# Expert rows weighted on eviction and added into the residual by scatter, in place of a gather and mix of chosen rows

## The chip, the cores and the metric

The program runs on one core of one Trainium2 chip, in float32 (some matmul operands are float32r or bfloat16). The metric is the device time of one execution in microseconds (us). The kernel before took 609.7 us, the median of three runs (607.96 to 610.41).

## The reference

The input is one sequence of 2048 tokens of width 128. Four residual blocks follow one another, each on a layer norm of the running sum:

```python
x = x + attn_a(layernorm(x))     # 16 heads, element-wise decaying state, a scan over the tokens
x = x + ffn(layernorm(x))        # mixture of experts, first pass
x = x + attn_b(layernorm(x))     # linear attention with exp features
x = x + ffn(layernorm(x))        # mixture of experts, second pass, same weights
```

The change is in `ffn`. It routes each token to 2 of 8 experts, each with room for 640 tokens; a token beyond that is dropped for that expert:

```python
logits = xt @ w_g
top_v, top_i = top_k(logits, 2)
probs  = softmax over the two chosen logits          # = sigmoid of their difference, both ways
rank   = running count of tokens per expert; kept if rank < 640
h      = gelu(batch[e] @ c_fc[e])                    # 640x128 @ 128x512
y      = h @ c_proj[e]                               # 640x512 @ 512x128
out[t] = sum over the (at most) 2 kept experts of probs * y[slot of t]
```

## The kernel before

Engine programs are written by hand, one list of instructions for each engine, and they meet at semaphores. The order on each queue is the order in the code. Tokens stand in 16 tiles of 128 (four chunks of four tiles); `xres` in SBUF is the running sum.

A pass of the mixture of experts (k = 0 or 1) goes so:

- **Routing.** For each chunk VectorE (DVE) picks the two experts (`choose`, which also writes `gap`, the difference of the two top logits), TensorE counts ranks, DVE makes slot numbers (`locate`).
- **Dispatch.** GpSimd (POOL) scatters the normed rows with 32 indirect DMAs (L447) into `slots_x[k]` in DRAM. A row holds 128 numbers and the number of the place in `chosen_y` where its result belongs. Slots that no token takes keep the number 65536, which the result's scatter skips.
- **Experts.** For each of 8 experts SyncE (SP) loads the 640 rows (`xe`), TensorE turns them and multiplies, ScalarE (ACT) does the Gelu, and DVE copies the result from PSUM to `ye` (L932). POOL scatters it with 5 indirect DMAs of 128 rows into `chosen_y` in DRAM (L477). `xe`, `ye` and `y_to` have two buffers.
- **Combination.** When all 80/2 = 40 scatters of the pass have landed, SP loads `chosen_y` back into `got` with 8 DMAs (L332), two for each chunk. DVE multiplies each tile of `got` by `weight` and adds it to `xres`, two instructions for each tile (`mix`, L941 and L946). `weight` comes from `probabilities` (ACT) and `weights` (DVE, with the matmul `totals`).

After pass 0 the second attention starts: `stats_chunk` and `norm_chunk` on DVE, `turn_chunk` (L1267) and `project` on TensorE, and then the features, where TensorE, ACT and DVE are all busy. ACT's features begin behind `act.wait_ge(mixed, NT)` (L670). After pass 1 SP waits for all of `mixed` and stores `xres` to `out` with one DMA (L356).

Of the kernel before, what the change touches and what calls it, by code (L numbers as in the profile page):

```python
# [46 lines left out]
ROW = D + 1  # L47
# [23 lines left out]
def program(nc, x, Wq, Wk, Wv, Wbeta, Wg, Wout, ln_g, ln_b, W_qkv, proj, W_out, b_out, w_g, c_fc, c_proj, out):  # L71
# [8 lines left out]
    with ctx:  # L80
# [29 lines left out]
        chosen_y = nc.dram_tensor("chosen_y", [KT * P, D], F32).ap()  # L110
# [38 lines left out]
        with ExitStack() as mb:  # L149
# [9 lines left out]
            gap = sb("gap", [P, NT], F32, mb)  # L159
            prob = sb("prob", [P, KT], F32, mb)  # L160
# [7 lines left out]
            limits = sb("limits", [P, NT, NE], F32, mb)  # L168
            limit = sb("limit", [P, NT], F32, mb)
            kept = sb("kept", [P, KT], F32, mb)  # L170
            weight = sb("weight", [P, KT], F32, mb)
# [7 lines left out]
            got = sb("got", [P, KT, D], F32, m)  # L179
            projf = got[0:3 * GR, 0:NT, :].rearrange("p (g t) d -> p g (t d)", g=NG)  # L180
# [24 lines left out]
        slots_clear, y_clear = sem("slots_clear"), sem("y_clear")  # L205
# [17 lines left out]
        logit_mm, logit_used, route_step, gap_ready, prob_ready = (  # L223
            sem(n) for n in ("logit_mm", "logit_used", "route_step", "gap_ready", "prob_ready"))
        chosen_ready, carry_ready, rank_mm, rank_used, index_ready, limit_mm, limit_used, weight_ready, scattered = (
            sem(n) for n in ("chosen_ready", "carry_ready", "rank_mm", "rank_used", "index_ready", "limit_mm",
                             "limit_used", "weight_ready", "scattered"))
# [4 lines left out]
        rows_made, ids_made, y_to_ready = sem("rows_made"), sem("ids_made"), sem("y_to_ready")  # L232
        got_in = [sem(f"got_in{c}") for c in range(NB)]
        mix_first = sem("mix_first")
        pstklo_ready = sem("pstklo_ready")
        mixed = sem("mixed")
# [17 lines left out]
        out_t = out.rearrange("a (t p) d -> p (a t) d", p=P)  # L254
# [18 lines left out]
        def _(sp):  # L273
# [21 lines left out]
            for j in range(0, KT, 4):  # L295
                sp.dma_start(chosen_y[j * P:(j + 4) * P, :].rearrange("(j p) d -> p j d", p=P),
                             empty_rows[:, 0:4, 0:D]).then_inc(y_clear, 16)

            def experts(k):

                if k == 0:
                    sp.wait_ge(xres_a, NB)
                else:
                    for c in range(NB):
                        sp.wait_ge(stk_in[c], 2 * 16 * 3 * NG)
                sp.dma_start(cfc_sb[:], c_fc.rearrange("e d f -> d e f")).then_inc(cfc_in, 16)
                if k == 0:
                    sp.wait_ge(zeroed, 2)
                    for r in range(3):
                        for a_ in range(GH):  # L310
                            row = GR * r + HD * a_
                            sp.dma_start(projf[row:row + HD, :, a_ * F:(a_ + 1) * F],
                                         proj.rearrange("(g a) d f -> a d g f", a=GH)[a_]).then_inc(proj_in, 16)
                sp.wait_ge(scattered, 16 * KT * (k + 1))
# [40 lines left out]
            sp.wait_ge(mixed, 2 * NT)  # L355
            sp.dma_start(out_t, xres[:]).then_inc(stored, 16)  # L356
# [4 lines left out]
        def _(pool):  # L361
            pool.memset(empty_rows[:, :, 0:D], 0.0)
            pool.memset(empty_rows[:, :, D:ROW].bitcast(I32), int(FAR)).then_inc(zeroed, 1)
# [72 lines left out]
            def experts(k):  # L436

                if k == 0:
                    pool.wait_ge(xres_a, 1)
                    pool.iota(rows_x[:, :, D].bitcast(I32), [[P, KT]], base=0,  # L440
# [30 lines left out]
                pool.wait_ge(y_clear, 16 * KT // 4)  # L471
                for e in range(NE):
                    b = e % 2
                    pool.wait_ge(y_to_ready, k * NE + e + 1)
                    pool.wait_ge(ye_ready, k * NE + e + 1)
# [18 lines left out]
        def _(act):  # L494
# [108 lines left out]
            def probabilities(k):  # L603
                act.wait_ge(gap_ready, NB * (k + 1))
                act.activation(prob[:, 0:NT], gap[:], ACT.Sigmoid).then_inc(prob_ready, 1)
                act.activation(prob[:, NT:KT], gap[:], ACT.Sigmoid, scale=-1.0).then_inc(prob_ready, 1)

# [4 lines left out]
            def experts(k):  # L612
                probabilities(k)
                for e in range(NE):
                    b = e % 2
                    s = k * NE + e
                    if s == 2:
                        stack_proj()
# [51 lines left out]
            act.wait_ge(mixed, NT)  # L670
# [33 lines left out]
        def _(dve):  # L704
# [115 lines left out]
            def choose(k, c, lg):  # L820
# [3 lines left out]
                for kk, src in enumerate((lg, lg2[:])):  # L824
# [5 lines left out]
                    if kk == 0:  # L830
# [7 lines left out]
                dve.tensor_tensor(gap[:, TB * c:TB * c + TB], top[:, 0, :], top[:, 1, :],  # L838
                                  ALU.subtract).then_inc(gap_ready, 1)
# [26 lines left out]
            def weights(k, totals):  # L866
                dve.wait_ge(limit_mm, k + 1)
                by_tile = chosen[:, :, 1, :, :].rearrange("p c e t -> p c t e")
                dve.tensor_tensor(limits[:].rearrange("p (c t) e -> p c t e", t=TB), by_tile,
                                  totals.unsqueeze(1).unsqueeze(1).broadcast_to((P, NB, TB, NE)),  # L870
                                  ALU.mult).then_inc(limit_used, 1)
                dve.wait_ge(limit_used, k + 1)
                link(dve.tensor_reduce(limit[:], limits[:], AX_X, ALU.add))
                dve.tensor_tensor(kept[:, NT:KT].rearrange("p (c t) -> p c t", t=TB), place[:, :, 3, :],
                                  limit[:].rearrange("p (c t) -> p c t", t=TB), ALU.is_ge)
                link(dve.tensor_single_scalar(kept[:, 0:NT].rearrange("p (c t) -> p c t", t=TB), place[:, :, 1, :],
                                              float(CAP), ALU.is_lt))
                dve.wait_ge(prob_ready, 2 * k + 2)
                dve.tensor_tensor(weight[:], prob[:], kept[:], ALU.mult).then_inc(weight_ready, 1)

# [24 lines left out]
            def experts(k, n):  # L905
                weights(k, ps[:, n, 2 * P:2 * P + NE])
# [10 lines left out]
                for e in range(NE):  # L917
# [9 lines left out]
                    if s >= 2:  # L927
                        dve.wait_ge(ye_out[b], 16 * NS * (s // 2))
                    dve.wait_ge(xe_in[b], 16 * (s // 2 + 1))
                    dve.tensor_copy(y_to[:, b, :], xe[:, b, :, D].bitcast(I32)).then_inc(y_to_ready, 1)  # L930
                    dve.wait_ge(ye_mm, s + 1)
                    dve.tensor_copy(ye[:, b, :], flat(ps[:, 6:8, :])[:, 0:NS * D]).then_inc(ye_ready, 1)  # L932

            def mix(k, c):
                if c == 0:
                    dve.wait_ge(weight_ready, k + 1)
                dve.wait_ge(got_in[c], 32 * (k + 1))

                def second(t):
                    dve.wait_ge(mix_first, k * NT + t + 1)  # L940
                    dve.scalar_tensor_tensor(out=xres[:, t, :], in0=got[:, NT + t, :],  # L941
                                             scalar=weight[:, NT + t:NT + t + 1], in1=xres[:, t, :],
                                             op0=ALU.mult, op1=ALU.add).then_inc(mixed, 1)

                for t in range(TB * c, TB * c + TB):
                    dve.scalar_tensor_tensor(out=xres[:, t, :], in0=got[:, t, :], scalar=weight[:, t:t + 1],  # L946
                                             in1=xres[:, t, :], op0=ALU.mult, op1=ALU.add).then_inc(mix_first, 1)
                    if t % TB:
                        second(t - 1)
                second(TB * c + TB - 1)  # L950

            experts(0, NB - 1)

            def stats_chunk(c):
                for t in range(TB * c, TB * c + TB):
                    dve.wait_ge(mixed, t + 1)
# [20 lines left out]
            mix(0, 0)  # L977
            stats_chunk(0)
            for c in range(NB):
                if c + 1 < NB:  # L980
                    mix(0, c + 1)
# [82 lines left out]
            experts(1, 5)  # L1064
            for c in range(NB):
                mix(1, c)
# [3 lines left out]
        def _(pe):  # L1070
# [137 lines left out]
            def totals(k, bank):  # L1208
                pe.wait_ge(carry_ready, (k + 1) * (NB + 1))
# [235 lines left out]
```

## Time and profile before

| | |
|---|---|
| median of three runs | 609.7 us (607.96 to 610.41) |
| the profiled execution | 607.78 us |
| its span in the profile | 606.1 us |
| busy: TensorE / VectorE / ScalarE / GpSimd | 390.6 / 301.9 / 237.9 / 225.7 us |
| chain of work that ended last | TensorE 41%, VectorE 13%, issue 8%, GpSimd 6%, ScalarE 5%, DMA 5% |
| eight experts of pass 0, first scatter to last landing | 236.9 to 309.3 us |
| eight experts of pass 1, first scatter to last landing | 515.5 to 588.0 us |

The profiled execution is 1.7 us longer than its span, and 1.9 us shorter than the median of the runs. Times in rows count from the start of the span. SPq is the queue on which SyncE issues DMAs. A DMA_INDIRECT row of POOL is the time in which it issues one scatter; the transfer comes behind it.

### The profile page before, as it was taken

To read this page: it belongs to the slowest core of one execution; us is meant where nothing else is said; L and a number is where in the kernel's file an instruction comes from. 1 tells how busy PE (TensorE), PEld (TensorE's weight loads), DVE (VectorE), ACT (ScalarE), POOL (GpSimd) and SP (SyncE) were. 2 spreads that over 40 slices of the span, in tenths; PEclk is the share of its full clock that TensorE was granted. 3 is DMA by queue.
4 is the path that set the end of the run, shared out by engine and by line. 5 is a ranking of instruction groups with operands and counts; after the bars stand their busy time and mean duration, and the time that the engine had idled before them with its cause. 6 is when DMAs were issued, how large, how long until landed. Compare 5 with 4: busy or idle time off the path is not lost.

```text
span 606.1 us, 6501 instructions
## 1 busy us (share of the span) xinstructions
PE 390.6 (64%) x2202; PEld 261.1 (43%) x2202; DVE 301.9 (50%) x711; ACT 237.9 (39%) x328; POOL 225.7 (37%) x245
## 2 busy tenths in 40 slices
PE   3737677557340029999807899975777209999920
PEld 2435444225230018888604533332444107888710
DVE  5486999837550001132139699878675501111105
ACT  2835333255240004323203799876745302332300
POOL 4002898800066692465423100000531550645540
PEclk9959897887555559999957999999775557999975
DMA  7950000000311121221051433330100120222016
GB/s 199 359 182 2 1 1 0 0 1 1 138 40 48 44 66 38 68 77 48 24 156 41 104 96 96 97 127 1 36 17 19 35 78 22 55 72 72 29 58 175
DMA packets 36289, 41.27 MB, mean 68 GB/s; under 512 B 5664, under 2 KB 23712, under 8 KB 36256
## 3 DMA queue, kind: packets, MB, share of 16 engines
q1 hardware_dynamic: 31648, 32.42, 18.4%
q0 software_dynamic: 4608, 8.44, 4.1%
q8 instruction: 18, 0.29, 0.2%
q14 instruction: 15, 0.12, 0.1%
HBM read 17.68 MB, written 17.90 MB: 59 GB/s over the span
## 4 chain that ended last, share of the span: by engine, by line
PE 41%; DVE 13%; issue 8%; POOL 6%; ACT 5%; DMA 5%; SPq 1%; POOLq 0%; DVEq 0%; ACTq 0%
PE ps L1072 38%; POOL slots_x L447 5%; DVE feat L997 3%; DMA slots_x<-rows_x,put_at 2%; PE ps L1223 2%; ACT expo L655 1%; DMA got<-chosen_y 1%; DVE xres L946 1%; DVE xres L941 1%; DMA xe<-slots_x 1%; DVE stats L807 1%; ACT rows_x L591 1%; ACT L655 1%; DMA chosen_y<-ye,y_to 1%; PE ps L1183 1%
## 5 line engine op out<-in xcount | busy, mean ns | idle before, releaser
L447 POOL DMA_INDIRECT slots_x<-rows_x,put_at x64 | 62.8, 981 | 166.1 <-DVE put_at L856 119.2
L477 POOL DMA_INDIRECT chosen_y<-ye,y_to x80 | 79.3, 992 | 94.2 <-DVE ye L932 68.3
L623 ACT ACTIVATE hT<-ps 128x640 f32<-128x640 f32 x64 | 45.0, 703 | 162.5 <-PE ps L1072 162.5
L997 DVE SCALAR_TENSOR_TENSOR feat<-expo,ps 128x1024 f32<-128x1024 f32 x64 | 76.8, 1216 | 11.5 <-ACT expo L655 11.1
L1072 PE MATMUL ps<-xeT,cfc_sb 128*128 128x320 f32 x256 | 75.8, 451 | 1.8 <-DVE xeT L914 1.8
L655 ACT ACTIVATE expo<-ps,minus_one 128x1024 f32<-128x1024 f32 x64 | 70.2, 1114 | 11.8 <-PE ps L1072 7.8
L1072 PE MATMUL ps<-cproj_sb,hT 128*128 128x128 f32 x640 | 74.6, 275 | 0.3
L1072 PEld LDWEIGHTS ps<-cproj_sb,hT 128*128 128x128 f32 x640 | 73.0, 192 | 0.9 <-ACT hT L623 0.6
L914 DVE COPY xeT<-ps 128x640 f32<-128x640 f32 x16 | 13.2, 824 | 120.0 <-PE ps L1223 120.0
L1072 PEld LDWEIGHTS ps<-xeT,cfc_sb 128*128 128x128 f32 x256 | 47.8, 199 | 24.0 <-ACT hT L623 6.5
L1223 PE MATMUL ps<-ident,xe 128*128 128x128 f32 x80 | 12.5, 292 | 57.0 <-DMA xe<-slots_x 57.0
L932 DVE COPY ye<-ps 128x640 f32<-128x640 f32 x16 | 13.2, 824 | 64.0 <-PE ps L1072 64.0
L424 POOL TENSOR_TENSOR read<-state,qT 128x1024 f32<-128x1024 f32 x16 | 38.1, 2379 | 9.9 <-DVE state L784 9.7
L784 DVE TENSOR_TENSOR_SCAN state<-decay,state,ps 128x1024 f32<-128x1024 f32 x16 | 37.5, 2343 | 0.9
L416 POOL TENSOR_TENSOR decay<-krep_sb,bkT 128x1024 f32<-128x1024 f32 x8 | 19.0, 2373 | 46.6 <-ACT krep_sb L548 46.6
L1223 PEld LDWEIGHTS ps<-ident,xe 128*128 128x128 f32 x80 | 10.4, 151 | 60.1 <-issue 57.2
L1072 PE MATMUL ps<-stk,pstk 97*128 97x512 f32 x64 | 24.0, 464 | 10.7 <-DVE feat L997 9.8
L541 ACT ACTIVATE decay<-decay 128x1024 f32<-128x1024 f32 x16 | 16.6, 1057 | 30.0 <-POOL decay L416 30.0
L1072 PE MATMUL ps<-feat,kvl 128*32 128x512 f32 x128 | 21.3, 742 | 7.0 <-DVE feat L997 6.9
L1072 PE MATMUL ps<-vhi,sel 128*128 128x512 f32 x32 | 16.2, 505 | 11.6 <-DVE state L784 11.5
L1072 PE MATMUL ps<-pstk,stk 97*128 97x512 f32 x64 | 22.9, 444 | 1.1 <-DVE part L974 0.8
L946 DVE SCALAR_TENSOR_TENSOR xres<-got,weight,xres 128x128 f32<-128x128 f32 x32 | 10.3, 343 | 24.3 <-DMA got<-chosen_y 24.3
(196 smaller groups left out, 634.5 us busy)
## 6 DMA issues: line engine op xcount, KB each, us to landing
stk<-part SPq DMA_DIRECT2D x96, 64.0 KB, 2.0
slots_x<-empty_rows SPq DMA_DIRECT2D x16, 322.5 KB, 6.9
xe<-slots_x SPq DMA_DIRECT2D x16, 322.5 KB, 3.0
cfc_sb<-in_L_ffn_c_fc SPq DMA_DIRECT2D x2, 2048.0 KB, 8.2
got<-chosen_y SPq DMA_DIRECT2D x16, 256.0 KB, 4.7
chosen_y<-empty_rows SPq DMA_DIRECT2D x8, 256.0 KB, 6.0
chosen_y<-ye,y_to POOLq DMA_INDIRECT x80, 2.2
xres<-in_L_attn_a_x SPq DMA_DIRECT2D x4, 256.0 KB, 3.9
```

Of the source, the lines that this page charges most:

```text
L416: pool.tensor_tensor(decay[:, n % ND, :], krep_sb[:], bkT[:, c * CH:(c + 1) * CH], ALU.mult).then_inc(product_pool, 1)
L424: pool.tensor_tensor(read[:, i, :], state[:, i, :], qT[:, c * CH:(c + 1) * CH], ALU.mult).then_inc(read_ready, 1)
L447: pool.indirect_dma_start(out=slots_x[k], out_offset=bass.IndirectOffsetOnAxis(ap=put_at[:, c, kk, t:t + 1], axis=0), in_=rows_x[:, kk * N ...
L477: pool.indirect_dma_start(out=chosen_y, out_offset=bass.IndirectOffsetOnAxis(ap=y_to[:, b, i:i + 1], axis=0), in_=ye[:, b, i * D:(i + 1) * ...
L541: act.activation(decay[:, n % ND, :], decay[:, n % ND, :], ACT.Identity, scale=-1.0, bias=1.0).then_inc(decay_ready, 1)
L623: act.activation(hT[:, b, f, :].rearrange("p (a n) -> p a n", a=2), ps[:, 2 + 2 * (f % 2):4 + 2 * (f % 2), 0:HALF], ACT.Gelu).then_inc(h_r ...
L655: act.activation(expo[:, g % 3, :], flat(ps[:, pair, :]), ACT.Exp, bias=minus_one[:]).then_inc(f_exp, 1)
L784: dve.tensor_tensor_scan(out=state[:, i, :], data0=decay[:, n % ND, :], data1=flat(ps[:, 2 + 2 * (n % 2):4 + 2 * (n % 2), :]), initial=sta ...
L946: dve.scalar_tensor_tensor(out=xres[:, t, :], in0=got[:, t, :], scalar=weight[:, t:t + 1], in1=xres[:, t, :], op0=ALU.mult, op1=ALU.add).t ...
L997: dve.scalar_tensor_tensor(out=feat[:, g % 4, :], in0=expo[:, g % 3, :], scalar=1.0, in1=flat(ps[:, pair, :]), op0=ALU.min, op1=ALU.max).t ...
L1072: return pe.matmul(o, lhsT, rhs, start=start, stop=stop, **kw)
L1223: ins = pe.transpose(ps[:, i // TB, (i % TB) * P:(i % TB + 1) * P], xe[:, b, i, 0:D], ident[:])
```

## The change

- `chosen_y`, `got`, `gap`, `prob`, `kept`, `weight` and what makes them go: `probabilities`, `weights`, `totals`, `mix`.
- A DRAM tensor `total[k]` for each pass holds 2048 rows of the residual and 640 spare rows. SP copies `xres` into it chunk by chunk when the chunk is complete (`keep_rows`).
- A row of `slots_x` is now 130 numbers: the last is the logit difference with the sign for this choice, written by two small DVE instructions for each chunk. The number before it is the token; an unused slot names a spare row.
- For each expert ACT takes tanh of half the difference for the 5 x 128 slots, DVE makes the weight 0.5 + 0.5 tanh of it, and the eviction of `ye` from PSUM is a multiplication by it.
- POOL's scatters add into `total[k]` in DRAM (`compute_op=ALU.add`). Two experts of one token must not add at once, so the scatters of an expert wait until those of the expert before it have landed.
- After pass 0 SP loads the four chunks of `xres` back from `total[0]`. After pass 1 one DMA copies `total[1]` from DRAM to `out`.

```diff
+            def keep_rows(k, c):
+                sp.dma_start(total[k][c * BK:(c + 1) * BK, :].rearrange("(t p) d -> p t d", p=P),
+                             xres[:, TB * c:TB * c + TB, :]).then_inc(total_in[k], 16)
...
                 if k == 0:
-                    sp.wait_ge(pstklo_ready, 1)
-                for c in range(NB):
-                    for kk in range(2):
-                        j = kk * NT + TB * c
-                        sp.dma_start(got[:, j:j + TB, :],
-                                     chosen_y[j * P:(j + TB) * P, :].rearrange("(j p) d -> p j d", p=P)
+                    for c in range(NB):
+                        sp.dma_start(xres[:, TB * c:TB * c + TB, :],
+                                     total[0][c * BK:(c + 1) * BK, :].rearrange("(t p) d -> p t d", p=P)
                                      ).then_inc(got_in[c], 16)
...
-            sp.wait_ge(mixed, 2 * NT)
-            sp.dma_start(out_t, xres[:]).then_inc(stored, 16)
+            sp.dma_start(out.rearrange("a (p r) d -> p (a r d)", p=P),
+                         total[1][0:TOK, :].rearrange("(p r) d -> p (r d)", p=P)).then_inc(stored, 16)
...
+                    if e:
+                        pool.wait_ge(ye_out[1 - b], 16 * NS * ((s + 1) // 2))
                     for i in range(NS):
                         pool.indirect_dma_start(
-                            out=chosen_y, out_offset=bass.IndirectOffsetOnAxis(ap=y_to[:, b, i:i + 1], axis=0),
-                            in_=ye[:, b, i * D:(i + 1) * D], in_offset=None, bounds_check=KT * P - 1,
-                            oob_is_err=False,
-                        ).then_inc(ye_out[b], 16)
+                            out=total[k], out_offset=bass.IndirectOffsetOnAxis(ap=y_to[:, b, i:i + 1], axis=0),
+                            in_=ye[:, b, i * D:(i + 1) * D], in_offset=None, bounds_check=TOK + CAP - 1,
+                            compute_op=ALU.add).then_inc(ye_out[b], 16)
...
+                    act.activation(slot_w[:, b, :], xe[:, b, :, D + 1], ACT.Tanh, scale=0.5).then_inc(share_ready, 1)
...
-            act.wait_ge(mixed, NT)
...
+                    dve.tensor_scalar(slot_w[:, b, :], slot_w[:, b, :], 0.5, 0.5, ALU.mult, ALU.add)
...
-                    dve.tensor_copy(ye[:, b, :], flat(ps[:, 6:8, :])[:, 0:NS * D]).then_inc(ye_ready, 1)
+                    dve.tensor_tensor(ye[:, b, :].rearrange("p (i d) -> p i d", i=NS),
+                                      flat(ps[:, 6:8, :])[:, 0:NS * D].rearrange("p (i d) -> p i d", i=NS),
+                                      slot_w[:, b, :].unsqueeze(2).broadcast_to((P, NS, D)),
+                                      ALU.mult).then_inc(ye_ready, 1)
```

GpSimd's queue at the first experts of pass 0, before. `ye_ready` and `y_to_ready` say that DVE has written an expert's rows and their places.

```order
L477 DMA chosen_y<-ye,y_to 4096x128 [waits y_to_ready,ye_ready,y_clear,stk_ones]
L477 DMA chosen_y<-ye,y_to 4096x128 x4
L477 DMA chosen_y<-ye,y_to 4096x128 [waits ye_ready,y_to_ready]
L477 DMA chosen_y<-ye,y_to 4096x128 x4
L477 DMA chosen_y<-ye,y_to 4096x128 [waits ye_ready,y_to_ready]
```

The same place in the changed program. `ye_out0` and `ye_out1` count landed scatters of the experts with an even and an odd number.

```order
L480 DMA total<-ye,y_to 2688x128 [waits y_to_ready,total_in0,ye_ready,spare_clear,stk_ones]
L480 DMA total<-ye,y_to 2688x128 x4
L480 DMA total<-ye,y_to 2688x128 [waits ye_out0,ye_ready,y_to_ready]
L480 DMA total<-ye,y_to 2688x128 x4
L480 DMA total<-ye,y_to 2688x128 [waits ye_out1,ye_ready,y_to_ready]
```

The number of scatters stays; from the second expert on the first of five also waits until the previous expert's five have landed.

SyncE's queue at the end of the program, before:

```order
L321 DMA xe<-slots_x 128x645 [waits y_to_ready,xe_turned] x6
L332 DMA got<-chosen_y 128x4x128 [waits ye_out1,ye_out0]
L332 DMA got<-chosen_y 128x4x128 x7
L356 DMA out<-xres 128x16x128 [waits mixed]
L80 UNCONDITIONAL_BRANCH [waits stored]
```

And in the changed program:

```order
L322 DMA xe<-slots_x 128x650 [waits y_to_ready,xe_turned] x6
L353 DMA out<-total 16x16384 [waits ye_out1,ye_out0]
L80 UNCONDITIONAL_BRANCH [waits stored]
```

The eight loads and the wait for DVE's mixing are gone, and the store waits for the scatters alone.

ACT's queue where the features of the second attention begin, before:

```order
L495 ACTIVATE part<-ps 128x512 [waits q2_mm]
L655 ACT_TABLE_LOAD [waits f_mm]
L655 ACTIVATE expo<-ps,minus_one 128x1024 [waits mixed]
L655 ACTIVATE expo<-ps,minus_one 128x1024 [waits f_mm] x2
```

And in the changed program:

```order
L497 ACTIVATE part<-ps 128x512 [waits q2_mm]
L649 ACT_TABLE_LOAD
L649 ACTIVATE expo<-ps,minus_one 128x1024 [waits f_mm] x3
```

The table load for the exponential no longer carries the wait for TensorE's first features; the exponential has it.

## Rows read from the trace of the kernel before

**Rows 1.** The page, busy time of each engine over the span.

```profile
PE 390.6 (64%) x2202; PEld 261.1 (43%) x2202; DVE 301.9 (50%) x711; ACT 237.9 (39%) x328; POOL 225.7 (37%) x245
```

**Rows 2.** Chain of waits, end of pass 1: start us, us, what.

```profile
578.93 0.83 DVE ye L932
...
585.72 2.24 DMA chosen_y<-ye,y_to
...
588.02 0.37 SPq L332
```

**Rows 3.** Timeline, SyncE's queue: start us, us, engine, line, instruction, count.

```profile
600.59 0.38 SPq L356 DMA_DIRECT2D out<-xres  x1
```

**Rows 4.** DMA queues and issues; the last number is median us to landing.

```profile
q0 software_dynamic: 4608, 8.44, 4.1%
...
cfc_sb<-in_L_ffn_c_fc SPq DMA_DIRECT2D x2, 2048.0 KB, 8.2
...
chosen_y<-ye,y_to POOLq DMA_INDIRECT x80, 2.2
...
out<-xres SPq DMA_DIRECT2D x1, 1024.0 KB, 5.1
...
wg_sb<-in_L_ffn_w_g SPq DMA_DIRECT2D x1, 4.0 KB, 1.9
```

**Rows 5.** Timeline of GpSimd, experts of pass 0; in brackets idle time before.

```profile
236.91 0.98 POOL L477 DMA_INDIRECT chosen_y<-ye,y_to  x1 [10.70 <-DVE ye L932]
...
246.20 0.98 POOL L477 DMA_INDIRECT chosen_y<-ye,y_to  x1 [3.17 <-DVE ye L932]
247.48 0.98 POOL L477 DMA_INDIRECT chosen_y<-ye,y_to  x1 [0.30 <-issue]
...
255.52 0.98 POOL L477 DMA_INDIRECT chosen_y<-ye,y_to  x1 [3.22 <-DVE ye L932]
...
301.97 0.98 POOL L477 DMA_INDIRECT chosen_y<-ye,y_to  x1 [3.06 <-DVE ye L932]
...
307.10 0.98 POOL L477 DMA_INDIRECT chosen_y<-ye,y_to  x1 [0.30 <-issue]
```

**Rows 6.** Timeline of GpSimd, dispatch of pass 1, around a wait for landed scatters.

```profile
481.87 0.98 POOL L447 DMA_INDIRECT slots_x<-rows_x,put_at  x1 [0.30 <-issue]
485.02 0.98 POOL L447 DMA_INDIRECT slots_x<-rows_x,put_at  x1 [2.17 <-DMA slots_x<-rows_x,put_at]
```

**Rows 7.** The chain of waits at the same place.

```profile
481.87 2.32 DMA slots_x<-rows_x,put_at
```

**Rows 8.** Timeline of all engines between pass 0 and the features.

```profile
309.39 5.35 SPq L332 DMA_DIRECT2D got<-chosen_y  x8
313.21 0.61 DVE L946 SCALAR_TENSOR_TENSOR xres<-got,weight,xres 128x128 f32<-128x128 f32 x2 [12.07 <-DMA got<-chosen_y]
...
315.32 0.86 DVE L957 BATCH_NORM_STATS2 stats<-xres 128x6 f32<-128x128 f32 x4
...
316.38 0.58 DVE L946 SCALAR_TENSOR_TENSOR xres<-got,weight,xres 128x128 f32<-128x128 f32 x2
316.50 0.30 ACT L583 ACTIVATE std<-mv,eps_col 128x4 f32<-128x4 f32 x1 [19.03 <-DVE mv L960]
...
318.46 0.17 DVE L965 RECIPROCAL rstd<-std 128x4 f32<-128x4 f32 x1
...
319.06 1.58 PE L1267 MATMUL ps<-ident,xn 128*128 128x128 f32 x4 [18.78 <-DVE xn L968]
...
330.55 1.30 PE L1267 MATMUL ps<-ident,xn 128*128 128x128 f32 x4
...
335.26 0.60 PE L1267 MATMUL ps<-ident,xn 128*128 128x128 f32 x4
...
340.22 1.63 PE L1072 MATMUL ps<-pstk,stk 97*128 97x512 f32 x6 [0.75 <-DVE part L974]
341.00 1.28 ACT L655 ACT_TABLE_LOAD   x1 [0.89 <-PE ps L1072]
```

More of the change, by code:

```diff
@@ L313, in experts @@
                                          proj.rearrange("(g a) d f -> a d g f", a=GH)[a_]).then_inc(proj_in, 16)
+                if k == 1:
+                    for c in range(NB):
+                        sp.wait_ge(xres_b, c + 1)
+                        keep_rows(1, c)
                 sp.wait_ge(scattered, 16 * KT * (k + 1))
@@ L837, in choose @@
                                        initial=0.0, op0=ALU.mult, op1=ALU.add).then_inc(chosen_ready, 1)
-                dve.tensor_tensor(gap[:, TB * c:TB * c + TB], top[:, 0, :], top[:, 1, :],
-                                  ALU.subtract).then_inc(gap_ready, 1)
+                for kk in range(2):
+                    dve.tensor_tensor(rows_x[:, kk * NT + TB * c:kk * NT + TB * c + TB, D + 1], top[:, kk, :],
+                                      top[:, 1 - kk, :], ALU.subtract)
             def begin_counts(k):
@@ L864, in locate @@
                 dve.wait_ge(carry_ready, k * (NB + 1) + c + 2)
[L866 to L879, printed above, removed]
             layer_norm(1, otok, otok)
@@ L903, in _, with experts @@
                     locate(0, c - 3, ps[:, c - 3, P:2 * P].rearrange("p (r t e) -> p r t e", r=4, e=NE))
-            def experts(k, n):
-                weights(k, ps[:, n, 2 * P:2 * P + NE])
+            def experts(k):
                 def turned_in(e):
@@ L928, in experts, with stats_chunk @@
                         dve.wait_ge(ye_out[b], 16 * NS * (s // 2))
+                    dve.wait_ge(share_ready, s + 1)
+                    dve.tensor_scalar(slot_w[:, b, :], slot_w[:, b, :], 0.5, 0.5, ALU.mult, ALU.add)
                     dve.wait_ge(xe_in[b], 16 * (s // 2 + 1))
                     dve.tensor_copy(y_to[:, b, :], xe[:, b, :, D].bitcast(I32)).then_inc(y_to_ready, 1)
+                    dve.wait_ge(y_to_ready, s + 1)
                     dve.wait_ge(ye_mm, s + 1)
-                    dve.tensor_copy(ye[:, b, :], flat(ps[:, 6:8, :])[:, 0:NS * D]).then_inc(ye_ready, 1)
[L934 to L943, printed above, removed]
-                for t in range(TB * c, TB * c + TB):
[L946 to L956, printed above, removed]
+                    dve.tensor_tensor(ye[:, b, :].rearrange("p (i d) -> p i d", i=NS),
+                                      flat(ps[:, 6:8, :])[:, 0:NS * D].rearrange("p (i d) -> p i d", i=NS),
+                                      slot_w[:, b, :].unsqueeze(2).broadcast_to((P, NS, D)),
+                                      ALU.mult).then_inc(ye_ready, 1)
+            experts(0)
+            def stats_chunk(c):
+                dve.wait_ge(got_in[c], 16)
+                for t in range(TB * c, TB * c + TB):
                     dve.bn_stats(stats[:, t, :], xres[:, t, :]).then_inc(ln_stat, 1)
@@ L1062, in _ @@
             locate(1, NB - 1, ranks_in(4))
-            experts(1, 5)
-            for c in range(NB):
-                mix(1, c)
+            experts(1)
         @block.tensor
@@ L1258, in _ @@
                     rank(0, c - 2, c - 2)
-            totals(0, NB - 1)
             experts(0)
@@ L1419, in _ @@
             rank(1, NB - 1, 4)
-            totals(1, 5)
             experts(1)
```

69 lines of the change are left out of this document (28 added, 41 removed).

## The prediction

> **What bounds the kernel now.** I began with busy time by engine [rows 1]: TensorE is busy for 64% of the span and nothing for more, so stages with different limits follow one another, and a change is worth what it takes from the wait that ends last in its stage. The chain of waits comes next, and there the stretches that the change touches. At the end of pass 1 the reader is to see that TensorE is done by 578.93, that the last scatter has landed at 585.72 + 2.24 = 587.96, and that the loads and the mixing on DVE keep the store back until 600.59 [rows 2, 3]. Nothing else is at work there, so this tail of 606.1 - 588.0 = 18.1 us is paid in full. After pass 0 the same loads and mixing stand between the last landing (SP issues at 309.39) and TensorE's next matmul at 319.06 [rows 8]. Between these, in both passes, GpSimd's timeline shows the experts: five scatters, 1.28 us apart, a gap of 3.2 us, five again; the period is 255.52 - 246.20 = 9.32 us, and DVE's `ye`, which follows TensorE, ends each gap [rows 5]. TensorE sets the pace of the experts and GpSimd has slack; the change spends that slack.
>
> **The change part by part.** All sums are against the profiled execution (607.8 us, span 606.1); the median of the runs is 1.9 us above it, and I add the differences to the median, 609.7.
>
> *The end of pass 1.* Before, from SP's first issue at 588.02 to landing of the store: the store is issued at 600.59 and takes 5.1 us [rows 3, 4], so it lands at 605.7. Now the store is issued at 588.02 (plus what the scatters lose, below) and copies 1 MB from DRAM to DRAM. No row shows such a copy. From below it is the store from SBUF, 5.1 us for the same bytes; from above the load of twice the bytes, 8.2 us [rows 4], since a copy in DRAM reads and writes 1 MB each. I take 6.5, between them. It lands at 594.5, which is 11.2 us less (between 12.6 and 9.5).
>
> *Between pass 0 and the second attention.* The first pair of loads is issued at 309.39, and DVE starts on it at 313.21, 3.8 us later [rows 8]. One load in place of two, one issue earlier (5.35/8 = 0.67 us): chunk 0 is there at about 312.5, and its statistics start then and not at 315.32, since the mix of chunk 0 is gone: 2.8 us. Then in the old order the mix of chunk 1 stood between the statistics (done at 316.38) and the reciprocal at 318.46, though ACT's root was done at 316.80. That saves 1.7 us more. TensorE starts at 319.06 - 4.5 = 314.6. From there to the first features at 340.22 it is TensorE that works or waits for its copies; only the turn of chunk 2 was stretched by rows that came one by one, 1.30 us against 0.60 for chunk 3, and that 0.7 us should go [rows 8]. The other mixes lie beside TensorE and give nothing. Last, the table load for the exponential stood behind TensorE's first features (341.00) and can now run 0.9 us earlier; TensorE's filler matmuls cover part of it, so I take 0.5 (between 0 and 0.9). Together -5.7 us. If less of this reached TensorE's start than I think, 2.8 us is the sure part.
>
> *The routing.* Two tiny DVE instructions in place of one for each chunk, before the first slot number. I take +0.15 us for each pass, +0.3; `weights`, `probabilities` and `totals` were off the chain, behind which GpSimd went on scattering, and give nothing.
>
> *Inside an expert.* The tanh (5 elements a partition) stands before the expert's four Gelus on ACT, and the 5-element DVE instruction before `y_to`. Both engines idle for most of a 9.32 us period here (by the gaps that end with it in GpSimd's timeline [rows 5], `ye` has to wait for TensorE each time). The eviction as a product has the same 640 elements as the copy of 0.83 us [rows 2]. I take nothing. The two table loads at the head of a pass stay two; the second comes after `xe` has landed, beside TensorE's turn and first products. `keep_rows` adds four DMAs of 256 KB a pass; SP's wait for them holds back only the loads of `xe`, which wait for all scatters of the dispatch anyway, and GpSimd's first result scatter comes only after the dispatch, those loads and a whole expert. Nothing.
>
> *The scatters.* This is the term that can eat the rest. Write s for the distance of two scatters (1.28) and L for issue start to landing of the last (2.24) [rows 2, 5]. With the new wait, GpSimd cannot begin expert e+1 before expert e has landed and the wait is through. The dispatch of pass 1 prices the waking [rows 6, 7]: landed at 481.87 + 2.32 = 484.19, next scatter at 485.02, so 0.83 us. The period of the serial chain is P = 4s + L + 0.83. At the price of plain scatters that is 5.13 + 2.24 + 0.83 = 8.2 us, below 9.32: the wait alone is hidden, with 1.1 us to spare. What is added to it is the addition. Below 9.32 a pass loses only its tail, 4 times the growth of s and the growth of L; above, 7 times the excess as well.
>
> No row shows an adding scatter. Below: the plain one, s = 1.28, L = 2.24; a gain is excluded, as the same five DMAs of 128 indices are made and more is read. Above for L: the read of the old row comes first as a transfer of its own, 1.9 us for a tiny load from DRAM [rows 4], L = 4.1. Above for s: GpSimd's 0.98 us doubles, s = 2.26. I take s = 1.38 and L = 2.8, near the plain row: a tiny load from DRAM (1.9) and a scatter into it (2.2) take much the same time, most of which must be fixed, and the second read can run beside the first; the software queue's 4608 packets fill 4.1% of 16 engines, 86 ns a packet and two packets an engine for each scatter [rows 4], so twice the reading is 0.2 us more. The dropped rows (a fifth of the slots) are now written too, for which GpSimd's time, one for each index, should not change. Then P = 5.5 + 2.8 + 0.83 = 9.15, just hidden, and a pass loses 0.4 + 0.56 = 0.96 us, both 1.9.
>
> The Trainium skill ("Collectives: The Full Stack", The bandwidth ceiling: the fold count and why AG ≠ RS ≠ AR) says that an addition in the DMA engine reads both operands with a descriptor each, and that such a transfer ran at half the rate of a plain one. For the data alone that is the 0.2 us that I have. But GpSimd writes the descriptors here ("DMA: Bandwidth & Descriptors", SWDGE vs HWDGE vs iDMA), and three for a row in place of two would speak for the rival below. No row here bears on it either way.
>
> *The sum.* -11.2 - 5.7 + 0.3 + 1.9 = -14.7 us: 593.1 for a profiled execution, 595.0 on the median.
>
> **The rivals.** *The serial scatters become the bound (the other side).* Place: GpSimd's wait for the previous expert, in both passes. It decides from 4s + L > 8.49. If GpSimd's busy part grows by half, 0.98 to 1.47, then s = 1.77, L = 2.24 + 0.49 + 0.17 = 2.9, P = 10.8. From first scatter to last landing a pass takes 7 x 10.8 + 7.1 + 2.9 = 85.6 us in place of 309.33 - 236.91 = 72.4, so 13.2 more, 26.5 for both. With -16.6 from the other parts this is +9.9: 619.6 us. For it speaks how near P is: a growth of s by 0.2 with L = 2.9 is enough to reach 9.32. Against it that GpSimd's time may be mostly fixed. At both upper ends (s = 2.26, L = 4.1) P is 14.0 and the time some 670 us.
>
> *Only the landing is long.* s stays and L is 4.1: P = 10.06, a pass takes 79.7 us, 7.2 more, both 14.5. Sum -2.1: 607.6 us, no change that can be told. What speaks against it is that a read and a write need not be one after the other for the queue as a whole.
>
> *The savings are mostly hidden.* The store from DRAM takes 8.2 us, and the second attention's start gives little (a load into `xres` lands as late as two did, or TensorE's slow first matmuls absorb it). That is +1.7 + 4.5 against the forecast: 601 us. The change then does less than it says, and it is still faster.
>
> **How the numbers follow.** Forecast 0.48; mostly hidden 0.10; only the landing 0.09; the serial bound 0.33. A measurement tells from no change what is beyond 0.5%, 3 us. Faster: 0.48 + 0.10 and a third of the landing case, 0.61. Within: 0.05 of the landing case and the border of the serial one, 0.07. Slower: 0.32. The forecast's own range is 591 to 601 (the bounds of the store and of the table load, no growth of the scatters at one end, one just past 9.32 at the other). The range that I give, 590 to 624, reaches over the landing case and the serial one at its price of a half more; what is left out are the upper ends of s and L.
>
> **What would show it.** The scatters' rows: distance 1.28 to 1.4, median landing below 3, and the gap before each first scatter released by `ye` on DVE, with a period of 9.32. If instead the gap is released by a DMA, or the period is above 9.4, the serial chain decides. The end: one store, issued within 0.1 us of the last landing, which ends 5 to 8 us later. After pass 0: 5 us from the last landing to TensorE's first turn in place of 9.7, and 20.5 us from there to the first features. I am wrong if s is above 1.5 or L above 3.2.

## The result and the profile after

The changed kernel takes 628.84 us (median of 4 runs, 627.72 to 633.1), the kernel before beside it on the same chip 608.83. The ratio is 1.036, with a 95% interval of 1.032 to 1.041: slower by 3.6%. The forecast was 595.0 us; the time lies 34 us above it and 5 us above the top of the range. The rival that came true is the one in which the serial scatters become the bound.

The profiled execution took 627.7 us, with a span of 625.5 us against 606.1. The page first, its busy times by engine (compare [rows 1]), the software queue's row of its list of DMA queues (compare [rows 4]), and the costliest group of GpSimd:

```profile
PE 392.1 (63%) x2200; PEld 261.0 (42%) x2200; DVE 286.2 (46%) x661; ACT 239.1 (38%) x340; POOL 271.7 (43%) x246
q0 software_dynamic: 13568, 9.51, 11.3%
L480 POOL DMA_INDIRECT total<-ye,y_to x80 | 125.5, 1568 | 87.4 <-DVE ye L919 32.5
```

TensorE is still the busiest. GpSimd has grown to 271.7 us, and its 80 result scatters take 125.5 us, 1568 ns each. The software queue carries 13568 packets in place of 4608.

Now the experts of pass 0 on GpSimd's timeline (columns as in [rows 5], the same place in the program):

```profile
237.87 1.59 POOL L480 DMA_INDIRECT total<-ye,y_to  x1 [12.65 <-DVE ye L919]
...
245.36 1.55 POOL L480 DMA_INDIRECT total<-ye,y_to  x1 [0.30 <-issue]
249.41 1.55 POOL L480 DMA_INDIRECT total<-ye,y_to  x1 [2.50 <-DMA total<-ye,y_to]
...
256.83 1.55 POOL L480 DMA_INDIRECT total<-ye,y_to  x1 [0.30 <-issue]
260.89 3.26 POOL L480 DMA_INDIRECT total<-ye,y_to  x1 [2.51 <-DMA total<-ye,y_to]
```

The first scatters of two experts stand 249.41 - 237.87 = 11.54 us apart, where it was 9.32, and the gap before the second is ended by a DMA and not by `ye`. (The 32.5 us that the page's group puts down to `ye` are the waits for the first expert of each pass, 12.65 and 19.89.) The chain of waits runs through the same landings (start, us, what):

```profile
245.36 3.21 DMA total<-ye,y_to
256.83 3.22 DMA total<-ye,y_to
...
304.63 3.23 DMA total<-ye,y_to
...
327.53 3.23 DMA total<-ye,y_to
330.83 2.76 DMA xres<-total
```

So s is (245.36 - 237.87)/4 = 1.87, later 1.855; L is 3.22; and the waking is 249.41 - 245.36 - 3.21 = 0.84. The period is 4 x 1.855 + 3.22 + 0.84 = 11.5.

One reading lesson lies in the timeline of all engines before the last expert but one, the seventh, of pass 0:

```profile
307.89 0.17 DVE L914 TENSOR_SCALAR slot_w<-slot_w 128x5 f32<-128x5 f32 x1 [10.38 <-DMA total<-ye,y_to]
307.97 0.16 DVE L916 COPY y_to<-xe 128x5 int32<-128x5 int32 x1
308.16 0.82 DVE L919 TENSOR_TENSOR ye<-ps,slot_w 128x640 f32<-128x640 f32 x1
308.71 1.55 POOL L480 DMA_INDIRECT total<-ye,y_to  x1 [2.52 <-DVE y_to L916]
```

GpSimd's gap is put down to DVE's `y_to`, as are nine of the fourteen gaps of both passes. But the landing at 304.63 + 3.23 = 307.86 released both: DVE 0.03 us later, GpSimd 0.85 us later, the same time as after every other landing. This `y_to` is not even the one that GpSimd needed. It is the last of the pass's eight copies and belongs to the eighth expert; the seventh's stands at 296.48, 12 us before. Of several waits only the last by the profile is named; where gaps of the same length have different names, look for what both waited for.

Compare the two stretches by their engines, from the first result scatter to the last one's issue in pass 0. First the kernel before, then after; columns: window, us, busy us of PE, PEld, DVE, ACT and POOL, granted clock, DMA share, GB/s.

```profile
237.00:309.00 72.00, 63.15 (x416) 53.32 (x414) 13.63 (x21) 22.07 (x30) 40.09 (x40) 0.98 0.18 53
```

```profile
238.00:330.00 92.00, 63.37 (x415) 53.08 (x414) 14.52 (x28) 22.80 (x35) 63.63 (x40) 0.86 0.37 47
```

TensorE does the same work in the same busy time (63 us), and 20 us go to waiting. Nearly all of this waiting comes at the end. After its last expert TensorE idles until the row at 319.06 before, for 18.78 us [rows 8], and until the row at 335.75 after, for 33.19 us (below). So it was done at 300.28 and is done at 302.56, only 2.3 us later, while GpSimd's last landing moved from 309.3 to 330.8. TensorE keeps its pace, and GpSimd falls behind it by some 2.2 us with each expert. The lower mean of the granted clock (0.86 against 0.98) follows from that: it was 1.00, the level of 2.4 GHz, from 238 to 300 us and 0.50, the level of 1.2 GHz, from 308.7 to 330, where TensorE had nothing to do.

What the change was to save is there. Between pass 0 and the features, and at the end of the program:

```profile
330.83 2.02 SPq L330 DMA_DIRECT2D xres<-total  x4
333.61 0.87 DVE L929 BATCH_NORM_STATS2 stats<-xres 128x6 f32<-128x128 f32 x4 [24.62 <-DMA xres<-total]
...
335.75 1.58 PE L1228 MATMUL ps<-ident,xn 128*128 128x128 f32 x4 [33.19 <-DVE xn L940]
```

```profile
616.75 1.54 POOL L480 DMA_INDIRECT total<-ye,y_to  x1 [0.30 <-issue]
620.10 0.55 SPq L353 DMA_DIRECT2D out<-total  x1
```

The span falls into five stretches, each from a row of the timelines (us, before and after):

| stretch | before | after | difference | predicted |
|---|---|---|---|---|
| start to first result scatter of pass 0 | 236.9 | 237.9 | +1.0 | +0.15 |
| pass 0, first scatter to last landing | 72.4 | 92.9 | +20.5 | +0.96 |
| last landing to first scatter of pass 1 | 206.2 | 198.4 | -7.8 | -5.5 |
| pass 1, first scatter to last landing | 72.4 | 90.9 | +18.5 | +0.96 |
| last landing to end | 18.1 | 5.4 | -12.7 | -11.2 |

The sum is +19.5, the growth of the span (+19.4) but for rounding. All of the miss is in the two rows of the experts. That the +1.0 of the first stretch is a price of the change is not shown. The first expert's 16 products on TensorE, right after some 40 us of idling, took 7.57 us, with the granted clock at 0.50 up to 228 us; in the trace before they took 5.95, with the clock at 1.00 from 228 us on. The kernel before with one wait added (below), whose program is the same up to there, shows 7.60 too. Against that the dispatch ended 1.0 us earlier in this trace (its last scatter at 211.17 against 212.15).

### The profile page after: what moved, and what is told of

Read it like the earlier page. It is cut to its first block, busy times and chain, and to the rows that moved or that the text cites. A ratio compares the mean times of both kernels' runs of the same rounds, so it can differ in the third digit from the quotient of the medians.

```text
span 625.5 us, 6474 instructions
## 1 busy us (share of the span) xinstructions
PE 392.1 (63%) x2200; PEld 261.0 (42%) x2200; DVE 286.2 (46%) x661; ACT 239.1 (38%) x340; POOL 271.7 (43%) x246
## 3 DMA queue, kind: packets, MB, share of 16 engines
q0 software_dynamic: 13568, 9.51, 11.3%
## 4 chain that ended last, share of the span: by engine, by line
PE 20%; issue 17%; POOL 17%; DVE 11%; DMA 9%; ACT 4%; POOLq 1%; SPq 1%; DVEq 0%; ACTq 0%
PE ps L1039 18%; POOL total L480 13%; DMA total<-ye,y_to 8%; POOL slots_x L446 3%; DVE feat L966 3%; ACT expo L655 1%; DVE stats L806 1%; ACT rows_x L593 1%; DMA slots_x<-rows_x,put_at 1%; DVE otok L718 1%; PE ps L1150 1%; SPq L309 1%; ACT xnT L497 1%; DVE stats L710 1%; DMA xe<-slots_x 0%
## 5 line engine op out<-in xcount | busy, mean ns | idle before, releaser
L480 POOL DMA_INDIRECT total<-ye,y_to x80 | 125.5, 1568 | 87.4 <-DVE ye L919 32.5
L966 DVE SCALAR_TENSOR_TENSOR feat<-expo,ps 128x1024 f32<-128x1024 f32 x64 | 77.0, 1217 | 10.8 <-ACT expo L655 6.8
L1186 PEld LDWEIGHTS ps<-ident,xe 128*128 128x128 f32 x80 | 10.3, 151 | 64.8 <-issue 60.5
L616 ACT ACTIVATE slot_w<-xe 128x5 f32<-128x5 f32 x16 | 3.3, 205 | 72.4 <-DMA xe<-slots_x 72.4
L543 ACT ACTIVATE decay<-decay 128x1024 f32<-128x1024 f32 x16 | 16.6, 1057 | 29.9 <-POOL decay L415 29.9
L919 DVE TENSOR_TENSOR ye<-ps,slot_w 128x640 f32<-128x640 f32 x16 | 13.2, 825 | 28.0 <-PE ps L1039 27.8
L914 DVE TENSOR_SCALAR slot_w<-slot_w 128x5 f32<-128x5 f32 x16 | 2.7, 166 | 48.4 <-DMA total<-ye,y_to 48.3
L1228 PE MATMUL ps<-ident,xn 128*128 128x128 f32 x16 | 3.4, 322 | 33.2 <-DVE xn L940 33.2
```

The costliest lines, as they stand in the source:

```text
L480: pool.indirect_dma_start(out=total[k], out_offset=bass.IndirectOffsetOnAxis(ap=y_to[:, b, i:i + 1], axis=0), in_=ye[:, b, i * D:(i + 1) * ...
L543: act.activation(decay[:, n % ND, :], decay[:, n % ND, :], ACT.Identity, scale=-1.0, bias=1.0).then_inc(decay_ready, 1)
L966: dve.scalar_tensor_tensor(out=feat[:, g % 4, :], in0=expo[:, g % 3, :], scalar=1.0, in1=flat(ps[:, pair, :]), op0=ALU.min, op1=ALU.max).t ...
L1186: ins = pe.transpose(ps[:, i // TB, (i % TB) * P:(i % TB + 1) * P], xe[:, b, i, 0:D], ident[:])
```

## The experiments

The theory after the result: an adding scatter costs GpSimd more than half again, and with the wait for the landing it makes a chain of 11.5 us an expert. Its rivals: the wait alone does it; the addition alone does it; some other part of the change (weights, `keep_rows`) slows the experts. Ratios are to the kernel before, timed beside each run.

**The changed kernel without the addition.** A second choice's row overwrites the first's.

```
-   in_=ye[...], in_offset=None, bounds_check=TOK + CAP - 1,
-   compute_op=ALU.add).then_inc(ye_out[b], 16)
+   in_=ye[...], in_offset=None, bounds_check=TOK + CAP - 1).then_inc(ye_out[b], 16)
```

> The changed kernel with plain scatters in place of adding ones (the second expert of a token overwrites instead of adding; the waits between experts stay). Theory A, the adding scatter is slow and the wait makes a serial chain of it: at the plain price, distance 1.28 and landing 2.24, the period 4 x 1.28 + 2.24 + 0.8 = 8.2 us lies under TensorE's 9.32, so the experts of a pass take 72.4 us again (92.9 and 90.9 in the changed kernel). Time 628.8 - 20.5 - 18.5 = 590 us, ratio to before 0.97. Theory B, the wait between experts is itself what costs, whatever the scatter: the period stays above 10 us, time above 610.

Measured: 592.62 us, ratio 0.974 [0.970, 0.978]. GpSimd's timeline in it:

```profile
240.33 1.00 POOL L480 DMA_INDIRECT total<-ye,y_to  x1 [12.55 <-DVE ye L918]
241.64 0.98 POOL L480 DMA_INDIRECT total<-ye,y_to  x1 [0.30 <-issue]
...
259.23 0.97 POOL L480 DMA_INDIRECT total<-ye,y_to  x1 [2.83 <-DVE ye L918]
```

Distance 1.28, and the gap ended by `ye` again. So it is, by `ye` or `y_to`, in eleven of the fourteen gaps of both passes. In pass 0 three were ended by a landing (after 4.0, 3.0 and 3.6 us, with 0.84 taken for the waking), and the pass took 73.3 us in place of 72.4; pass 1 took 72.4. Everything else in the change is worth 609.11 - 592.62 = 16.5 us; the prediction's other terms sum to 16.6. The addition alone turns a gain of 2.6% into a loss of 3.6%.

**The kernel before with the wait alone.**

```
+   if e:
+       pool.wait_ge(ye_out[1 - b], 16 * NS * ((k * NE + e + 1) // 2))
```

> The kernel before with one thing added: GpSimd waits before an expert's scatters until the previous expert's have landed. Theory A: period 8.2 us under 9.32, each wait is over before the rows are ready; no change, 608.8 +- 2 us, and the first scatter of each expert is still released by the eviction. Theory B: slower by 8 waits a pass of 1 to 2 us each, 620 to 640.

Measured: 609.48 us, ratio 1.000 [0.997, 1.004]. The wait is free with plain scatters, as the formula had it (8.2 < 9.32). It decides in three of the seven gaps of pass 0, where a landing was late, and in none of pass 1; the pass took 311.4 - 238.7 = 72.7 us, so nothing came of it. The first of the three is at the second expert, and the third expert was released by `ye` again:

```profile
243.84 0.98 POOL L479 DMA_INDIRECT chosen_y<-ye,y_to  x1 [0.30 <-issue]
248.94 0.98 POOL L479 DMA_INDIRECT chosen_y<-ye,y_to  x1 [4.12 <-DMA chosen_y<-ye,y_to]
...
257.76 0.98 POOL L479 DMA_INDIRECT chosen_y<-ye,y_to  x1 [2.71 <-DVE ye L934]
```

248.94 - 0.84 - 243.84 = 4.3 us for that landing, against the usual 2.24; by the same working the other two took 2.6 and 3.4 us. What delayed them was not tested.

**The kernel before with adding scatters, without the wait.** They add onto cleared rows, a tensor for each pass, so the result is the same.

```
-   out=chosen_y, ...
+   out=chosen_y[k], ...
-   oob_is_err=False,
+   oob_is_err=False, compute_op=ALU.add,
```

> The kernel before with adding scatters onto zeros, each pass in its own cleared tensor, so that nothing but the kind of scatter changes; no wait between experts. Theory A: GpSimd needs 5 x 1.86 = 9.3 us for an expert, just TensorE's 9.32, and with no wait nothing is serial: a pass loses only its tail, 4 x 0.57 + 1.0 = 3.3 us, both 6.5; 615 us, ratio 1.01. Theory C, adding scatters are slow in themselves and pile up in the DMA engines: landing grows from scatter to scatter, time over 625.

Measured: 615.98 us, ratio 1.011 [1.006, 1.015].

```profile
244.59 1.55 POOL L478 DMA_INDIRECT chosen_y<-ye,y_to  x1 [0.30 <-issue]
246.45 1.56 POOL L478 DMA_INDIRECT chosen_y<-ye,y_to  x1 [0.30 <-issue]
...
310.23 1.56 POOL L478 DMA_INDIRECT chosen_y<-ye,y_to  x1 [0.30 <-issue]
```

There is no gap left in pass 0 (in pass 1 it is 0.06 us an expert): GpSimd issues 40 scatters back to back, 5 x 1.86 = 9.3 us an expert, just the pace of TensorE. In this form the addition costs 6.9 us.

**The kernel before with both.** The two edits above together.

> The kernel before with both things, adding scatters onto cleared tensors and the wait for the previous expert: the fourth corner beside before (608.8), the wait alone (609.5) and the addition alone (616.0). If the loss comes from the two together, as the serial chain says, the period is 4 x 1.86 + 3.2 + 0.85 = 11.5 us and the passes take some 92 us in place of 72.4: 608.8 + 39 = 648 us. If the costs simply add up, it is 616.7.

Measured: 647.82 us, ratio 1.065 [1.059, 1.070].

```profile
237.19 1.60 POOL L480 DMA_INDIRECT chosen_y<-ye,y_to  x1 [10.85 <-DVE ye L935]
...
244.72 1.55 POOL L480 DMA_INDIRECT chosen_y<-ye,y_to  x1 [0.30 <-issue]
248.82 1.56 POOL L480 DMA_INDIRECT chosen_y<-ye,y_to  x1 [2.54 <-DMA chosen_y<-ye,y_to]
```

This closes the square: wait 1.000, addition 1.011, both 1.065. Alone they cost 0.4 and 6.9 us, together 38: the loss is neither the wait nor the addition but their sum in one period, 248.82 - 237.19 = 11.6 us here and 11.5 in the changed kernel.

**The changed kernel with the chain cut in two.** Odd experts add into a second tensor, and each expert waits only for the last but one. The odd experts' rows are not brought together with the rest.

```
-   pool.wait_ge(ye_out[1 - b], 16 * NS * ((s + 1) // 2))
+   pool.wait_ge(ye_out[b], 16 * NS * (s // 2))
-   out=total[k], ...
+   out=(total, other)[b][k], ...
```

> The changed kernel with the scatters of odd experts added into a second tensor, so that an expert waits only for the one before the previous (the results of the odd experts are then not combined with the rest). Theory A: the chain is gone, the period is TensorE's 9.32 or GpSimd's 9.3, a pass takes 65.1 + 7.4 + 3.2 = 75.7 us in place of 92.9 and 90.9; time 628.8 - 17.2 - 15.2 = 596 us. Theory C: adding scatters pile up by themselves, time above 615 as before.

Measured: 598.55 us, ratio 0.981 [0.978, 0.985]. The first rows of the second and third expert:

```profile
249.48 1.55 POOL L488 DMA_INDIRECT other<-ye,y_to  x1 [0.30 <-issue]
...
258.75 1.55 POOL L488 DMA_INDIRECT total<-ye,y_to  x1 [0.30 <-issue]
```

With the adding scatters unchanged and only the landing taken out of the period it is 258.75 - 249.48 = 9.27 us. Against the changed kernel 30 us are back, in a kernel that leaves out bringing the two tensors together.

**Scatters of 64 rows.** The changed kernel, adding in pass 0 and plain in pass 1; half of the rows are left out.

```
-   ap=y_to[:, b, i:i + 1] ... in_=ye[:, b, ...] ... compute_op=ALU.add)
+   ap=y_to[0:64, b, i:i + 1] ... in_=ye[0:64, b, ...] ... **({} if k else {"compute_op": ALU.add}))
```

> The changed kernel with scatters of 64 rows in place of 128 (half of the experts' rows are left out), adding in pass 0 and plain in pass 1. It asks what GpSimd's time for a scatter hangs on. If it is a fixed time plus a time for each row, the adding one falls from 1.55 us towards 1.0 and the plain one from 0.98 towards 0.7, and the difference of 0.57 halves. If it is fixed for the kind of instruction, both stay (1.55 and 0.98). With the first, the period of pass 0 is 4 x 1.3 + 2.5 + 0.8 = 8.5, hidden behind TensorE's 9.32, and with the second it stays above 10.5.

Measured, in a single execution: 604.1 us. First pass 0, then pass 1:

```profile
239.81 1.47 POOL L480 DMA_INDIRECT total<-ye,y_to  x1 [12.61 <-DVE ye L919]
...
246.74 1.41 POOL L480 DMA_INDIRECT total<-ye,y_to  x1 [0.30 <-issue]
250.50 1.40 POOL L480 DMA_INDIRECT total<-ye,y_to  x1 [2.36 <-DMA total<-ye,y_to]
...
529.06 0.92 POOL L480 DMA_INDIRECT total<-ye,y_to  x1 [0.30 <-issue]
```

Half of the rows take 1.40 us in place of 1.55, and 0.92 in place of 0.98. By a straight line through the two sizes (an estimate), the adding scatter has a fixed part of 1.25 us and 2.3 ns a row, the plain one 0.86 us and 0.9 ns a row. The addition costs 0.57 us at 128 rows, of which 0.39 is there whatever the rows. Fewer rows do not save this chain: the period is still 250.50 - 239.81 = 10.7 us. The software queue's packets in this run are 3200 for the 40 adding scatters of pass 0, 80 each, and 1280 for the 40 plain ones of pass 1, 32 each.

**Unused slots name no row.** The changed kernel; the empty slots (a fifth) carry an index beyond the tensor.

```
-   iota(empty_rows[:, :, D] ..., [[1, NS]], base=TOK, channel_multiplier=NS)
+   memset(empty_rows[:, :, D:D + 1] ..., int(FAR))
-   bounds_check=TOK + CAP - 1,
+   bounds_check=TOK + CAP - 1, oob_is_err=False,
```

> The changed kernel with unused slots naming no row, as in the kernel before, so that a fifth of the rows is skipped and not added to spare rows. If GpSimd's time goes by index, distance and time stay: 1.86 and 628 us. If it goes by rows that are really moved, the distance falls to 1.75 and the period to 11.1, 7 x 0.4 less a pass: 623 us. Landing may fall by 0.1 either way.

Measured: 633.23 us, ratio 1.040 [1.035, 1.046]. The distance of two scatters stays 1.86 us, the landing takes 3.2 to 3.4 us (3.15 to 3.30 in the changed kernel), the period is 11.5 to 11.7, and the queue's packets are as many:

```profile
q0 software_dynamic: 13568, 8.48, 10.3%
```

The bytes fall from 9.51 to 8.48 MB, the time does not. That it is longer than the changed kernel's is not shown: the interval of that ratio, 1.032 to 1.041, overlaps this one. An index costs GpSimd the same whether its row is written or not.

**Weights on eviction, plain scatters, additions by chunk.** From here on the aim is a kernel that beats both. It keeps the weight on eviction, scatters plain rows without a wait into a tensor of its own for each pass, loads both choices and adds them to the residual on DVE; `out` is stored chunk by chunk. The whole computation is done.

```
-   out=total[k], ..., compute_op=ALU.add
+   out=chosen_y[k], ..., oob_is_err=False
+   def mix(k, c):
+       dve.wait_ge(got_in[c], 32 * (k + 1))
+       rows = flat(xres[:, TB * c:TB * c + TB, :])
+       dve.tensor_tensor(rows, flat(got[:, TB * c:TB * c + TB, :]), rows, ALU.add)
+       ...
+       dve.tensor_tensor(rows, flat(got[:, NT + TB * c:NT + TB * c + TB, :]), rows, ALU.add)
```

> A version meant to beat both: weights on eviction and row weights as in the change, but plain scatters without waits into a tensor of chosen rows for each pass (both cleared at the start), 8 loads, and on DVE two adds of a whole chunk (128x512, 0.6 us each) in place of eight small ones (2.1 us); the store goes out chunk by chunk. Theory A: experts take 72.4 us a pass as before. Pass 0 saves about 2 us on the first chunk and 1 for the second chunk's mix; the tail after pass 1 is 5.9 us of load issue and landing, 1.2 of adds and 2.7 of the last store, 10 in place of 18. Sum -11: 598 us, ratio 0.982. Rival: clearing 2 MB more or the loads' contention takes it back, 605 and more.

Measured: 602.44 us, ratio 0.990 [0.986, 0.993]: faster than both, by less than expected. The end of pass 1 in it:

```profile
587.48 5.81 SPq L326 DMA_DIRECT2D got<-chosen_y  x8
591.03 0.69 DVE L923 TENSOR_TENSOR xres<-got,xres 128x512 f32<-128x512 f32 x1 [11.81 <-DMA got<-chosen_y]
...
594.05 0.69 DVE L923 TENSOR_TENSOR xres<-got,xres 128x512 f32<-128x512 f32 x1 [1.60 <-DMA got<-chosen_y]
...
596.02 0.69 DVE L923 TENSOR_TENSOR xres<-got,xres 128x512 f32<-128x512 f32 x1 [0.55 <-DMA got<-chosen_y]
```

The additions wait for loads; the tail is 601.7 - 587.4 = 14.3 us, between 18.1 before and 5.4 with the rows summed in DRAM.

**The same with the second choice's loads issued by ACT.**

```
+   act.dma_start(got[:, NT + TB * c:..., :], chosen_y[k][...])
```

> The version before with the loads of the second choices issued from ScalarE's queue beside SyncE's. The issue of eight loads falls from 5.4 us to 2.7. If issue limits the loads, pass 1's tail is 2 us shorter and pass 0's first chunk comes 0.6 us sooner: 595.5 us. If the transfers limit them (2 MB at what the queues move, as 8.2 us for a 2 MB load suggests), both versions are equal within 1 us.

Measured: 602.38 us, ratio 0.989 [0.986, 0.993], no different from the last. The issue after pass 1 took 2.2 us in place of 5.8, so the issue is not what limits them; the loads then take 5.8 us each (median, 5.0 in the last version).

**The same with a partition's rows side by side.** Pieces of 2 KB in place of 512 bytes.

```
-   chosen_y[k][...].rearrange("(j p) d -> p j d", p=P)
+   chosen_y[k][...].rearrange("(p j) d -> p j d", j=TB)
```

> The version with plain scatters and two adds a chunk, loads on two queues, and now with the chosen rows of a partition side by side in DRAM, so that a load moves 2 KB in a piece and not 512 B (four times fewer pieces). There the second to fourth chunk came 2 to 3 us apart though the issue took 0.6, so the transfers limit. If it is the number of pieces, the last chunk lands 2 to 3 us sooner after pass 1, and the time is 599.5 us, ratio 0.985. If it is the bytes, or the stores that run beside the loads, it stays at 602.4.

Measured: 604.42 us, ratio 0.990 [0.986, 0.993]. The loads take 4.9 to 5.0 us in place of 5.8, and the tail after pass 1 is 12.9 us in place of 13.9 in its trace, but the ratio stays what it was. Where the 3 us between this tail and the 10 expected go stays open.

## Why the prediction was wrong

*The tail.* Right in what goes, and 1.5 us better in size: -12.7 where -11.2 was predicted. The copy from DRAM to DRAM takes 5.0 us by the trace's list of DMA issues, the lower bound (a store from SBUF, 5.1), not the 6.5 taken; in four other runs that end with this copy it takes 5.3 to 5.6.

*Between pass 0 and the features.* Right: from the last landing to the features it was 30.9 us and is 25.1, -5.8, where -5.2 was predicted; 5.0 us to TensorE's first turn (5 predicted). The table load stands 0.9 us earlier against the features and gave its 0.5 on top (ACT's copy of the keys and values comes 0.56 us sooner behind the features), and another 1.4 us of the stretch came from places that I did not price.

*The routing and inside an expert.* The run without the addition gives the sum of all terms but the scatters: 16.5 us saved, 16.6 predicted. That this agrees to 0.1 us is in part luck. In its trace the start is 3.4 us longer (240.33 against 236.91), which no term of mine holds, pass 0 is 0.9 longer, the middle 9.0 and the tail 12.0 shorter. Between 1.0 and 3.4 us of difference at the start, most of it the slower first expert and a dispatch that ends at 211.2 to 213.7, the 0.15 us taken for the routing of pass 0 can't be seen.

*The wait.* Right: its formula (4s + L + 0.83), its threshold (9.32, which fits the free wait at 8.2 and the periods of 10.7 and 11.5 that were paid) and its price at plain scatters (nothing) held; the waking was 0.84.

*The scatters.* This step failed: "I take s = 1.38 and L = 2.8, near the plain row". Measured: s = 1.86, L = 3.22. So the four distances and the landing of a period, 8.3 us in my sum, are 10.6. The argument was that "most of which must be fixed" and that an addition therefore adds only data, 0.2 us. The first half is right, and it speaks the other way: the fixed part itself grows, by 0.39 us a scatter, as the straight line through the two sizes has it (an estimate). The 0.2 us stood on twice the packets, and this was wrong too: each adding scatter has 144 packets where a plain one had 32 (13568 - 4608 = 8960, over 80 scatters 112 more), and 80 with half of the rows, so one for each row and 16 more. The three-for-two descriptors that were named as what would speak for the rival are borne out in direction only. Of the 0.98 us by which the landing grew, 0.57 is the longer issue itself, since it counts from the start of the issue. What GpSimd does in the longer issue no run shows. The Trainium skill's half rate for additions ("Collectives: The Full Stack", The bandwidth ceiling: the fold count and why AG ≠ RS ≠ AR) says nothing of this issue time; by the trace the landing grew by a factor of 1.44 and GpSimd's time by 1.58, and it is the latter that is paid four times in each period.

*What the wrong size did.* The term is not linear. Up to a period of 9.32 it costs 2 us in all, above it seven times the excess in each pass. With the measured s and L the rival's working gives 7 x 11.5 + 7.42 + 3.22 = 91.1 us a pass; pass 1 took 90.9, and pass 0 took 92.9, since one scatter took 3.26 us (at 260.89) where the others took 1.55. The rival as priced (P = 10.8, 619.6 us) had the mechanism and was short by 0.7 us a period. Its decision point, 4s + L = 8.49, was within 1.1 us of the plain scatters' value and 0.2 us of the values that I took. The measured value is 10.6.

*The chances.* With bounds of 1.28 to 2.26 for s and 2.24 to 4.1 for L, most of the span between the bounds lies above 8.49: the middle is 4 x 1.77 + 3.17 = 10.3. I took values near one end on an argument without a row, so the forecast's 0.48 was too much and the range's top was too low.

## What to carry to other kernels

When a change makes an overlapped step serial, work out the period of the chain (issue, landing, waking) and set it against the pace of its stage; if the bounds of an unmeasured price straddle that threshold, give the far side a chance by its share of the span between the bounds unless a row says otherwise, and let the range reach its price, for the excess is multiplied by the number of periods. A wait and a dearer operation that are each free or nearly so can cost 6% together, so they are to be tried together. A running sum in DRAM saves its loads and mixing (16.5 us here), but here that was lost as long as each expert's additions waited for those before. Cut in two, the chain was gone, though no run that brings the two tensors together shows what is left of the gain; plain scatters with two additions by chunk kept 1% with the whole computation done.

## What the runs showed of the hardware

- An indirect scatter of 128 rows of 512 bytes costs GpSimd 0.98 us plain and 1.55 us adding, and lands in 2.24 and 3.22 us; with 64 rows GpSimd's time is 0.92 and 1.40 us. A plain one makes 32 packets with 128 rows and with 64, an adding one 144 and 80.
- Indices beyond the tensor save bytes (9.51 to 8.48 MB) and no time on GpSimd (1.86 us apart either way).
- A copy of 1 MB within DRAM landed in 5.0 to 5.6 us over five runs, near the store of 1 MB from SBUF, 5.1 us [rows 4].
- Single late landings occur with plain scatters in pass 0, where 2.24 us is usual: by the gaps of the two runs with plain scatters and the wait, 4.0 and 4.3 us at the first expert, 3.0 and 2.6 at the third, 3.6 and 3.4 at the fifth. A serial chain has to absorb them. The adding scatters of the changed kernel show none (3.15 to 3.30 us).
- The granted clock after 40 us without a matmul is 0.50; it reached 1.00 within the first expert's products, and when it did so moved the first result by 1.65 us between two runs of the same instructions up to there.
